# A three-stage float32 kernel on one core: paired probability-value products, other PSUM banks for the output tiles, smaller first loads, and a reordered first head

## What is computed

```
x = x + xattn(_layernorm(x), ctx_4096, ctx_4096)   # 32 query heads, 8 key/value heads, head size 128
x = x + attn(_layernorm(x))                        # 32 heads of size 16
x = x + ffn(_layernorm(x))                         # base product + 8 gated rank-16 experts
```

```
queries = _rope((q @ Wq.T) split in 32 heads);  keys = _rope((k @ Wk.T) split in 8 heads);  values = v @ Wv.T
scores = queries @ keys.T * 128 ** -0.5, causal;  attn = softmax(scores);  ctx = attn @ values
return ctx @ Wd.T                                  # Wd is 512 x 4096
```

## Time and profile before

| | |
|---|---|
| median of 3 runs | 716.91 us (716.67 to 1846.62) |
| the profiled execution | 717.73 us, span 715.7 us |
| PE busy | 705.5 us, 99% of the span, 4848 matmuls |
| DVE, POOL, ACT busy | 512.8, 472.1, 372.8 us |
| HBM | 40.04 MB read, 10.49 MB written, mean 71 GB/s |
| PE's share of the chain that ended last | 86% |

### The profile page before, as it was taken

The page is one execution under the profiler, slowest core; times in us unless marked ns, Lnnn a source line. Parts: engine busy times, 40 slices in busy tenths (PEclk is TensorE's granted clock), DMA queues, the critical chain, the costliest instruction groups (busy, mean ns, idle before and its releaser), DMA issues.

```text
span 715.7 us, 12890 instructions
## 1 busy us (share of the span) xinstructions
PE 705.5 (99%) x4848; PEld 563.6 (79%) x4848; DVE 512.8 (72%) x814; ACT 372.8 (52%) x559; POOL 472.1 (66%) x360
## 2 busy tenths in 40 slices
PE   8999999899999999999999999999999999999998
PEld 6788878677778788787778778777788888887886
DVE  5665897957857857757767767758667888889735
ACT  5555665644644643743743743743336677765220
POOL 1898145777776877867867867844624889985730
PEclk9999999999999999999999999999999999999999
DMA  7554513411310310311301301300300110011003
GB/s 273 207 166 144 170 51 103 162 49 41 118 45 16 117 44 19 113 43 42 103 31 44 103 29 60 104 1 16 103 0 2 45 31 31 2 41 50 16 1 117
DMA packets 25560, 51.08 MB, mean 71 GB/s; under 512 B 2352, under 2 KB 10672, under 8 KB 25520
## 3 DMA queue, kind: packets, MB, share of 16 engines
q1 hardware_dynamic: 25520, 50.53, 21.5%
HBM read 40.04 MB, written 10.49 MB: 71 GB/s over the span
## 4 chain that ended last, share of the span: by engine, by line
PE 86%; DVE 6%; ACT 2%; DMA 2%; issue 2%; POOL 1%; SPq 0%; DVEq 0%; ACTq 0%
PE pj L1583 11%; PE sc L1674 11%; PE pj L1674 10%; PE pj L1773 9%; PE tp L1583 8%; PE pv L1661 5%; PE sc L1641 4%; PE tp L1674 4%; PE pj L1951 3%; PE pv L1569 3%; PE sc L1823 2%; PE tp L1836 2%; PE pv L1847 2%; PE tp L1557 2%; PE pj L1557 2%; PE tp L1648 2%
## 5 line engine op out<-in xcount | busy, mean ns | idle before, releaser
L494 POOL TENSOR_TENSOR sw<-sw,cst 128x512 f32<-128x512 f32 x72 | 102.4, 1422 | 39.5 <-ACT sw L671 39.4
L518 POOL TENSOR_TENSOR sm<-sm,mx 128x512 f32<-128x512 f32 x64 | 72.0, 1131 | 40.7 <-DVE mx L1209 27.3
L523 POOL TENSOR_TENSOR sm<-sm,rz 128x512 f32<-128x512 f32 x64 | 66.7, 1057 | 24.1 <-DVE rz L1224 24.1
L500 POOL TENSOR_TENSOR qr<-t,sw 128x512 f32<-128x512 f32 x54 | 73.5, 1362 | 7.7
L1583 PE MATMUL tp<-x,w 128*128 128x512 f32 x288 | 76.3, 401 | 1.2 <-ACT sw L671 0.8
L793 ACT ACTIVATE sm<-sm 128x512 f32<-128x512 f32 x64 | 40.3, 633 | 61.9 <-POOL sm L518 61.9
L512 POOL TENSOR_TENSOR w<-raw,w 128x896 fp32r<-128x896 f32 x24 | 50.4, 2120 | 33.1 <-ACT w L656 33.1
L1773 PE MATMUL pj<-xh,ws 128*128 128x512 f32 x192 | 64.6, 402 | 0.2 <-ACT kb L891 0.2
L1583 PEld LDWEIGHTS tp<-x,w 128*128 128x128 f32 x288 | 51.9, 188 | 11.8 <-ACT sw L671 1.0
L656 ACT ACTIVATE w<-raw 128x1792 fp32r<-128x1792 f32 x15 | 25.6, 1707 | 59.8 <-DVE raw L1099 59.8
L1228 DVE TENSOR_TENSOR cl<-pv,ch 128x1024 fp32r<-128x1024 f32 x32 | 39.1, 1222 | 23.2 <-ACT ch L801 23.2
(11 more groups left out here) (274 smaller groups left out, 1850.4 us busy)
## 6 DMA issues: line engine op xcount, KB each, us to landing
rawd<-in_w_d SPq DMA_DIRECT2D x16, 512.0 KB, 3.2
raw<-in_w_q SPq DMA_DIRECT2D x15, 512.0 KB, 3.3
kscr<-sm SPq DMA_DIRECT2D x16, 256.0 KB, 2.1
vscr<-sm SPq DMA_DIRECT2D x16, 256.0 KB, 2.6
kr<-kscr SPq DMA_DIRECT2D x8, 512.0 KB, 3.3
vv<-vscr SPq DMA_DIRECT2D x16, 256.0 KB, 2.6
raw<-in_w_k SPq DMA_DIRECT2D x4, 512.0 KB, 6.2
cT<-in_ctxT SPq DMA_DIRECT2D x4, 512.0 KB, 7.2
```

Source lines behind the costliest of these rows:

```text
L494: pool.tensor_tensor(bs(sw[par][:, :]), bs(sw[par][:, :]), rep(cst[:, C_SIN:C_SIN + S], HB), ALU.mult).then_inc(sin_done, 1)
L500: pool.tensor_tensor(o, bs(t1[par][:, :]), bs(sw[par][:, :]), ALU.add).then_inc(rope, 1)
L518: pool.tensor_tensor(s3, s3, per_group(mx[:, c, :], 8), ALU.subtract).then_inc(subbed, 1)
L523: pool.tensor_tensor(s3, s3, per_group(rz[:, c, :], 8), ALU.mult).then_inc(normed, 1)
```

## The change

- `WARM_UP` goes from 16 to 9. The first piece of Wk comes in two loads of 256 KB, the first token half of the context in four of 256 KB; the second piece of Wk and the constants now stand ahead of the second token half. The first key tile takes its products chunk by chunk of the context, the low x high ones last, with semaphores of their own; ACT and DVE rotate the first two key tiles earlier in their order.
- Before the first head ACT swaps the second tile ahead of `block_hi(6)`, DVE does both `c_add` ahead of both `first_t1`.
- In each head g = 0 to 6 the two chunks of a half go through `pv_x` one right behind the other, the first into pv, the second into sc. The output tiles that stood in sc are now in pv; tile 4 is in B_BANK. The second transposes come one product earlier; ACT's copies and splits and DVE's `c_lo` are put in the matching order. The next head's scores now wait for the last `c_lo` and not for `out_add`.
- In the first head DVE sums the next queries' tile and multiplies by the cosine ahead of `sum_rec`, and the two `w7_lo` (128 x 896 each) come later.

The arithmetic is the same.

```diff
--- before.py
+++ after.py
@@ -34,7 +34,7 @@
-WARM_UP = 16
+WARM_UP = 9
@@ -119,7 +119,7 @@
-        wk = [sb(p1, f"wk{i}", [P, 2, KT, 256], F32R) for i in range(2)]
+        wk = [sb(p1, f"wk{i}", [P, 2, 2 * KT, P], F32R) for i in range(2)]
@@ -204,7 +204,8 @@
-        s_ctx = [sem(f"s_ctx{i}") for i in range(4)]
+        s_ctx = [sem(f"s_ctx{i}") for i in range(KT + 2)]
+        s_wa, phi_a, plo_a = sem("s_wa"), sem("phi_a"), sem("plo_a")
@@ -269,8 +270,8 @@
-        O_BANK = [B_BANK, sc[:, 0, :], sc[:, 1, :], B_BANK, sc[:, 0, :], sc[:, 1, :], B_BANK, C_BANK]
-        O6_BANK = [B_BANK, sc[:, 0, :], sc[:, 1, :], B_BANK, sc[:, 0, :], A_BANK, B_BANK, C_BANK]
+        O_BANK = [B_BANK, pv[:, 0, :], pv[:, 1, :], B_BANK, B_BANK, pv[:, 0, :], pv[:, 1, :], C_BANK]
+        O6_BANK = [B_BANK, pv[:, 0, :], pv[:, 1, :], B_BANK, B_BANK, A_BANK, B_BANK, C_BANK]
@@ -344,9 +345,9 @@
-            def load_ctx(half, i):
+            def load_ctx(s, k, n, half):
                 c = slice(half * HALF, (half + 1) * HALF)
-                sp.dma_start(cT[:, 2 * i:2 * i + 2, c], ctxT[:, 2 * i:2 * i + 2, c]).then_inc(s_ctx[2 * half + i], 16)
+                sp.dma_start(cT[:, k:k + n, c], ctxT[:, k:k + n, c]).then_inc(s_ctx[s], 16)
@@ -374,13 +375,14 @@
-            load_piece(0)
-            load_ctx(0, 0)
-            load_ctx(0, 1)
+            sp.dma_start(raw2[0][:, 0:512], w_k[0][:, 0:512]).then_inc(s_wa, 16)
+            for k in range(KT):
+                load_ctx(k, k, 1, 0)
+            sp.dma_start(raw2[0][:, 512:1024], w_k[0][:, 512:1024]).then_inc(s_w[0], 16)
             load_piece(1)
-            load_ctx(1, 0)
-            load_ctx(1, 1)
             sp.dma_start(cst[:, :], consts).then_inc(s_const, 16)
+            for i in range(2):
+                load_ctx(KT + i, 2 * i, 2, 1)
@@ -662,9 +664,17 @@
-                    if k % 2 == 0:
-                        act.wait_ge(s_ctx[2 * half + k // 2], 16)
+                    if half == 0:
+                        act.wait_ge(s_ctx[k], 16)
+                    elif k % 2 == 0:
+                        act.wait_ge(s_ctx[KT + k // 2], 16)
...
+            def first_hi(i, loaded, s):
+                act.wait_ge(loaded, 16)
+                hi(raw2[0][:, i * 512:(i + 1) * 512].rearrange("p (k c) -> p k c", k=KT),
+                   wk[0][:, 0, i * KT:(i + 1) * KT, :], s)
@@ -708,12 +718,16 @@
-            piece_hi(0)
+            first_hi(0, s_wa, phi_a)
             ctx_hi(0, range(KT))
+            first_hi(1, s_w[0], phi)
...
+            swap_k(0)
             piece_hi(2)
-            for t, i in PHASE1:
+            swap_k(1)
+            piece_hi(3)
+            for t, i in PHASE1[2:]:
@@ -724,8 +738,6 @@
-                    if i == 0:
-                        piece_hi(3)
@@ -769,8 +781,8 @@
+            first_swap(1, T_BANK)
             block_hi(6)
-            first_swap(1, T_BANK)
@@ -819,27 +831,25 @@
-                    part_copy(u2, 14 * n + 3, A_BANK)
-                    p_copy(q, 0)
-                    part_copy(pc, 14 * n + 4, C_BANK)
-                    exp(q + 2, 2, X_SCALE)
-                    wdhi(g, 1, wdh)
...
-                    wdhi(g, 1, wdh)
+                    p_copy(q, 0)
                     part_copy(u2, 14 * n + 3, A_BANK)
-                    exp(q + 2, 2, X_SCALE)
+                if first:
+                    part_copy(u2, 14 * n + 3, A_BANK)
                     p_copy(q, 0)
-                    part_copy(pc, 14 * n + 4, C_BANK)
+                part_copy(pc, 14 * n + 4, C_BANK)
+                p_copy(q + 1, 1)
+                exp(q + 2, 2, X_SCALE)
...
+                wdhi(g, 1, wdh)
                 turn(0, 1)
-                p_copy(q + 1, 1)
+                c_hi(q + 1, 1, sc4)
...
-                c_hi(q + 1, 1)
@@ -851,18 +861,16 @@
+                p_copy(q + 3, 3)
...
-                p_copy(q + 3, 3)
+                c_hi(q + 3, 3, sc4)
                 turn(1, 2)
-                if not more:
-                    turn(1, 3)
-                c_hi(q + 3, 3)
+                turn(1, 3)
                 if more:
-                    turn(1, 3)
@@ -1129,21 +1137,35 @@
-            piece_lo(0)
...
+            def first_lo(i, ready, s):
+                dve.wait_ge(ready, 1)
+                k = slice(i * KT, (i + 1) * KT)
+                dve.tensor_tensor(wk[0][:, 1, k, :], raw2[0][:, i * 512:(i + 1) * 512].rearrange("p (k c) -> p k c", k=KT),
+                                  wk[0][:, 0, k, :].bitcast(F32), ALU.subtract).then_inc(s, 1)
...
+            first_lo(0, phi_a, plo_a)
             ctx_lo(0, range(KT))
+            first_lo(1, phi, plo_d)
+            dve.wait_ge(s_const, 16)
+            t1_k(0)
             ctx_lo(1, range(KT))
+            t1_k(1)
             piece_lo(2)
-            dve.wait_ge(s_const, 16)
-            for ki in range(NKT):
+            t1_k(2)
+            piece_lo(3)
+            for ki in range(3, NKT):
...
-                if ki in (0, 3, 8, 9, 11):
-                    piece_lo({0: 3, 3: 4, 8: 5, 9: 6, 11: 7}[ki])
+                if ki in (3, 8, 11):
+                    piece_lo({3: 4, 8: 5, 11: 7}[ki])
...
+                if ki == 9:
+                    piece_lo(6)
@@ -1182,6 +1204,7 @@
+            for p in range(2):
@@ -1198,8 +1221,8 @@
+            w7_sum(3)
             first_add(7, 7)
-            w7_sum(3)
@@ -1262,33 +1285,37 @@
-                sum_rec(q, 0)
-                c_mix(0, 0)
                 if first:
+                    c_mix(0, 0)
                     t1_q(0, 0)
+                    sum_rec(q, 0)
                     sum_rec(q + 1, 1)
-                    w7_lo(3, 1, 0)
-                    w7_lo(3, 1, 1)
...
+                    sum_rec(q, 0)
+                    c_mix(0, 0)
...
-                if not first:
-                    wd_split(g, 0, wdh, wdl)
+                wd_split(g, 0, wdh, wdl)
...
-                    wd_split(g, 0, wdh, wdl)
+                    w7_lo(3, 1, 0)
                 c_lo(q, 0)
-                wd_split(g, 1, wdh, wdl)
-                t1_q(0, 2)
+                if first:
+                    t1_q(0, 2)
+                    wd_split(g, 1, wdh, wdl)
+                    w7_lo(3, 1, 1)
+                else:
+                    wd_split(g, 1, wdh, wdl)
+                    t1_q(0, 2)
...
+                c_lo(q + 1, 1, sc4)
                 out_add(g, 0)
-                c_lo(q + 1, 1)
@@ -1306,11 +1333,11 @@
+                c_lo(q + 3, 3, sc4)
...
-                c_lo(q + 3, 3)
@@ -1530,31 +1557,44 @@
-                piece, c = g // 2, slice(g % 2 * P, (g % 2 + 1) * P)
+                piece = g // 2
...
-                if piece == 1:
-                    pe.wait_ge(plo_p, 1)
-                elif ki:
-                    pe.wait_ge(plo_d, (1, None, 4, 5)[piece])
-                if h == 1:
+                def low():
+                    if piece == 1:
+                        pe.wait_ge(plo_p, 1)
+                    elif ki:
+                        pe.wait_ge(plo_d, (1, None, 4, 5)[piece])
+                    else:
+                        pe.wait_ge(plo_a, 1)
...
+                if ki == 4:
+                    pe.wait_ge(chi, 2 * KT)
+                elif h == 1:
...
-                    order = [(k, part) for part in (0, 2, 1) for k in range(KT)]
+                    order = [(k, part) for k in range(KT) for part in (0, 2)] + [(k, 1) for k in range(KT)]
+                    pe.wait_ge(phi_a, 1)
+                elif ki == 4:
+                    order = [(k, part) for k in range(KT) for part in (0, 2)] + [(k, 1) for k in range(KT)]
+                elif ki < 3:
+                    order = [(k, part) for k in range(KT) for part in (0, 1)] + [(k, 2) for k in range(KT)]
+                    pe.wait_ge(phi, piece + 1)
+                else:
+                    low()
                 for n, (k, part) in enumerate(order):
-                    if ki == 0:
-                        if n == 0:
-                            pe.wait_ge(phi, 1)
-                        if n == KT:
-                            pe.wait_ge(plo_d, 1)
-                        if part < 2:
-                            pe.wait_ge((chi, clo)[part], k + 1)
+                    if ki == 0 and part < 2:
+                        pe.wait_ge((chi, clo)[part], k + 1)
+                    if ki == 4 and part == 1:
+                        pe.wait_ge(clo, KT + k + 1)
+                    if ki < 3 and k == 0 and part == 2:
+                        low()
                     a, r = ((0, cxh), (0, cxl), (1, cxh))[part]
-                    last = pe.matmul(k_bank[ki % 4], w[:, a, k, c], r[:, k, tok],
+                    last = pe.matmul(k_bank[ki % 4], w[:, a, g % 2 * KT + k, :], r[:, k, tok],
@@ -1627,12 +1667,10 @@
-            def scores_x(g, j, held=False):
+            def scores_x(g, j):
...
-                else:
-                    pe.wait_ge(x_done, XD0 + 8 * g - 3 + (0 if held else c))
@@ -1648,17 +1686,15 @@
-            def pv_x(g, j):
```

(45 more changed lines are left out.)

16 lines of the change are left out of this document (9 added, 7 removed).

## The result

The changed kernel takes 707.31 us (median of 706.06, 706.25, 708.36 and 709.12), the kernel before 717.06 in the same session. That median still counts one disturbed execution of 1846.62 us; without it, it is 716.91. The ratio, 0.9868 with a 95% interval of 0.9835 to 0.9900, leaves that execution out. The forecast was 704.5 with a range of 702.0 to 709.0; the measured time lies in that range, but outside the 703.0 to 706.2 that the prediction gave as the forecast itself. The profiled execution took 706.25 us with a span of 704.3, against 717.73 and 715.7: 11.4 us less by the spans, where the forecast's terms add up to 12.4. So the total came out near, but in part by luck: its terms were wrong in both directions and the errors partly cancel.

The account below looks back on a forecast made before the run. PE, busy 705.5 of 715.7 us, was taken as the bound. Terms 5.6 + 2.5 + 0.4 + 1.2 + 3.1 - 0.4 = 12.4 us left 705.3 of 717.73; with the median 0.8 lower, 704.5 us, range 702.0 to 709.0.

Parts of the forecast that it names:

- Pairs: Heads 0 to 6: each half loses one of two visits to the 64-row products, 14 x 0.40 = 5.6 us gained.
- rival 2: ACT queue in the loop: ACT 1.8 late, PE waits 0.8 in six heads, 5 us back, 709.5; chance 0.10.
- rival 4: The pairs don't pair: second product pays the same change of bank or tile, 5.6 back, 710.1; chance 0.05.
- Start: Smaller first loads bring the context earlier, so key tile 1 starts at 9.1 instead of 11.56: 2.5 us gained.
- Rival 3: Start: the loads land no earlier, 2.5 us back, 707.0; chance 0.10.
- Tile 5 and the waits before the first head: K phase wait for ACT's swap goes, 0.4 us; two waits for ACT and DVE before head one go, 1.2 us.
- First head: DVE's new order shrinks PE's three waits: 3.6 us less 0.5 left for what is late next, 3.1 us gained.
- Head 6 to 7: Last rotation some 0.6 later behind c_lo and c_hi, PE 0.4 earlier, 0.6 to spare: 0.4 us lost.
- Rival 1: Warm-up too short, so the clock rises late: 2.0 us back, 706.5; chance 0.11.
- The last 0.8 us: Whole kernel: median of the runs put 0.8 below the profiled execution, taking 705.3 to the forecast 704.5 us.

## Why the prediction came out as it did

- *Pairs: right in mechanism, too small in size.* Forecast 0.40 a visit, measured 0.45 in a loop head, and 0.25 a head from the rest. A candidate for part of the latter: before, the two products ahead of `pv_x` took 3.15 us from start to start, now 3.05, and ACT's copy for the second one ended just as it started. A wait under 0.16 us has no bracket, so this is argued, not shown. No wait for ACT's swap: rival 2 is out, as is rival 4.
- *Start: 1.5 instead of 2.5.* The step that failed is the landing of the five small loads: I took the rates of large loads, by which 1.31 MB are through at 5.7 us. Small ones moved 298 GB/s, and by the changed kernel's slices 1.31 MB are through only at 6.5. The last piece reached ACT at 7.90, outside my 6.0 to 7.4; in the other profiles with these loads it came at 7.09 to 8.27. Rival 3 (no earlier at all) was wrong by 0.8 us for the context, and I missed PE's own order, worth 0.7.
- *Tile 5 and the waits before the first head*: gone. From tile 1 to the first head 2.3 us were gained against 1.6 in the first profile, 1.1 in the second; the surplus of the one was not traced.
- *First head: the step that failed.* I took the sum of the old waits, 3.6 us, as the gain and left 0.5 for what is late next. I had named the right instructions (the second Wd split and `w7_lo` in front of PE's first output tile and second half) but priced them alone, not beside POOL. At 2.2 us each instead of 1.21 they gave waits of 0.67, 1.18 and 0.43. By itself the new order cost 0.5 or more; the longest of the old waits, 1.35 + 0.16, was removed by the pairs' rearrangement already.
- *Head 6 to 7*: -0.4 forecast, a wait of 0.40 for `qr` measured; head 6 became 0.6 shorter where 0.8 - 0.4 = 0.4 was forecast.
- *The clock.* Rival 1 exists, in the profiled execution of one experiment. It isn't shown for the long runs of the changed kernel; in its second profile the rate rose 1.7 us later than in the first, and tile 1 still started 0.6 earlier.
- *The last 0.8 us*, by which I put the median under the profiled execution, went the other way: the profile fell on a short execution, the median is 1.1 above it. Of the 2.8 us between forecast and median, 1.9 are this and 0.9 the sum of the terms.
- *What was luck.* The first head's 2.7 us too many and the start's 1.0 were covered in part by the pairs' surplus and by 0.7 between tile 1 and the first head. Without the loop's surplus of 1.75 the median would have been 709.1, just outside the range.

## What to carry to other kernels

When a DVE instruction with both operands in SBUF is moved, price it by what POOL does at the new place, not by its time at the old one: here 1.21 us became 2.2. A term for waits that go away must be worked out as the next-latest arrival, not as the sum of the brackets; here the next arrivals took back 2.7 of 3.1 us, while the longest of the old waits would have gone without the new order. And a wait with thin cover can show as spread between executions: the stretch from tile 1 to the first head took 107.0 us in one profile of the changed kernel and 108.3 in the other.

## What was not expected of the hardware

- On DVE, an instruction with both operands in SBUF took 1.21 us alone and 2.17 to 2.31 where a POOL instruction was running when it started; it ended 0.95 to 1.07 us after POOL's. Where DVE's began first (128.34), it took 1.22, and POOL's took 1.96 instead of 1.05. A DVE instruction that read PSUM took 0.68 (`t`) and 1.21 (`cl`) either way.
- Around the context's 256 KB transfers the queue moved 298 to 310 GB/s from 2.1 to 6.3 us, with 512 KB ones 329 to 340.
- By the spacing of the matmuls TensorE went to 2.4 GHz at 13.5 us in one execution and at 8.9 in the one with four warm-up products, at 5.0 and 6.7 in the two of the changed kernel. The later rise of these two cost nothing that shows: tile 1 started at 9.45 there, at 10.07 in the other.
